# Expert layer: the 64-token tiles of two experts in one output tile, and weights loaded by pairs

## The reference, cut to what matters

```
dispatch   = jnp.einsum('sec,sd->ecd', sec_mask.astype(tokens.dtype), tokens)   # 16 x 320 x 128
h          = jax.nn.gelu(jnp.einsum('ecd,edf->ecf', dispatch, w1))              # w1: 16 x 128 x 512
expert_out = jnp.einsum('ecf,efd->ecd', h, w2)                                  # w2: 16 x 512 x 128
out        = jnp.einsum('sec,ecd->sd', combine_weights.astype(tokens.dtype), expert_out)
```

## Time and profile before

| | before |
|---|---|
| median of 3 runs | 884.03 us (880.08 to 884.72) |
| the profiled execution | 883.63 us |
| its span | 881.9 us |
| TensorE busy | 775.9 us, 88% of the span |
| VectorE, ScalarE, GpSimd busy | 527.1, 467.3, 306.0 us |
| DMA | 78.05 MB, mean 89 GB/s |
| second products L919, matmul passes | 384 records |
| weight loads of the expert stage | 24 transfers of 256 KB |

### The profile page before, as it was taken

One profiled execution on the slowest core, in us unless ns is written; L12 is line 12 of the kernel. 1 busy time (PEld: TensorE's weight loads), 2 busy tenths in 40 slices (PEclk: granted clock), 3 DMA queues, 4 the chain that ended last, 5 costly groups with the idle time before them and its releaser, 6 DMA issues.

```text
span 881.9 us, 19604 instructions
## 1 busy us (share of the span) xinstructions
PE 775.9 (88%) x7317; PEld 439.1 (50%) x7317; DVE 527.1 (60%) x1390; ACT 467.3 (53%) x743; POOL 306.0 (35%) x444
## 2 busy tenths in 40 slices
PE   1689999999928999479999999999999999999993
PEld 0234444444316777424555555555555555565441
DVE  4448888888441122255776647776665876545666
ACT  1487898889811222125544435554444555455575
POOL 3122443343337000234444325443334433224405
PEclk9999999999958999769999999999999999999997
DMA  1276333333205544131443244543335444222003
GB/s 28 75 236 157 105 98 103 106 101 97 64 31 130 153 141 140 54 89 49 103 100 71 52 88 103 103 102 72 70 73 96 103 91 92 56 55 54 2 1 96
DMA packets 111706, 78.05 MB, mean 89 GB/s; under 512 B 12272, under 2 KB 103088, under 8 KB 111616
## 3 DMA queue, kind: packets, MB, share of 16 engines
q1 hardware_dynamic: 106256, 70.38, 33.1%
q0 software_dynamic: 3344, 5.56, 2.5%
q10 hardware_dynamic: 2016, 0.92, 0.4%
HBM read 37.86 MB, written 13.63 MB: 58 GB/s over the span
## 4 chain that ended last, share of the span: by engine, by line
PE 34%; SPq 9%; DVE 6%; DMA 3%; issue 2%; ACT 1%; POOL 1%; ACTq 0%; DVEq 0%; POOLq 0%
PE l_ps_v L1287 7%; PE l_ps_c L1260 7%; SPq L115 4%; SPq L113 4%; PE l_ps_v L1188 4%; PE l_ps_d L1273 3%; PE l_by_query L1209 2%; DMA q_ring<-l_max_rows 2%; DVE l_rden L1839 2%; PE l_by_query L1200 2%; PE l_by_key L1242 1%; DVE l_neg_max L1827 1%; PE l_by_key L1380 1%; PE l_ps_m L1177 1%; PE l_ps_m L1380 1%
## 5 line engine op out<-in xcount | busy, mean ns | idle before, releaser
L1827 DVE TENSOR_REDUCE l_neg_max<-l_by_query 128x6 bf16<-128x768 f32 x125 | 119.7, 957 | 126.3 <-PE l_by_query L1213 125.6
L2107 POOL TENSOR_SCALAR_AFFINE_SELECT l_probs<-l_probs 128x512 f32<-128x512 f32 x128 | 88.2, 689 | 202.7 <-ACT l_probs L1533 202.4
L1533 ACT ACTIVATE l_probs<-l_by_key 128x768 f32<-128x768 f32 x128 | 103.8, 811 | 69.6 <-PE l_by_key L1245 65.4
L490 ACT ACTIVATE l_probs<-l_ps_s,minus_bound 128x1024 f32<-128x1024 f32 x128 | 137.2, 1118 | 2.4 <-PE l_ps_s L364 2.3
L1260 PE MATMUL l_ps_c<-l_probs,l_values 128*64 128x256 f32 (+1 forms) x1024 | 112.0, 340 | 0.0
L1260 PEld LDWEIGHTS l_ps_c<-l_probs,l_values 128*64 128x64 f32 x1024 | 62.3, 136 | 38.8 <-issue 19.6
L379 PE MATMUL l_ps_o<-l_probs,l_vpad 128*32 128x256 f32 x1024 | 78.9, 390 | 0.2 <-ACT l_probs L490 0.2
L1188 PE MATMUL l_ps_v<-w_v,l_xT 128*128 128x512 f32 x128 | 73.6, 657 | 0.4 <-ACT l_values L1554 0.4
L1554 ACT ACTIVATE l_values<-l_ps_v 128x512 f32<-128x512 f32 x64 | 38.2, 597 | 66.9 <-PE l_ps_v L1188 64.5
L1287 PE MATMUL l_ps_v<-w_o,l_ctx 128*128 128x128 f32 x512 | 66.9, 285 | 0.0
L2115 POOL DMA_INDIRECT l_eg<-eout_d,fetch x32 | 34.4, 1076 | 90.3 <-POOLq L836 82.7
(11 more groups left out here) (263 smaller groups left out, 1438.0 us busy)
## 6 DMA issues: line engine op xcount, KB each, us to landing
l_rrep<-rden_d SPq DMA_DIRECT2D x32, 512.0 KB
q_ring<-l_parts SPq DMA_DIRECT2D x192, 64.0 KB
k_ring<-l_parts SPq DMA_DIRECT2D x180, 64.0 KB
w_both<-in_L_ffn_w_dram SPq DMA_DIRECT2D x32, 256.0 KB, 3.1
disp_d<-zeros SPq DMA_DIRECT2D x8, 320.0 KB, 3.5
l_xin<-in_L_attn_x_dram SPq DMA_DIRECT2D x16, 128.0 KB, 2.5
l_xr<-in_L_attn_x_dram SPq DMA_DIRECT2D x16, 128.0 KB, 2.4
x_d<-l_x SPq DMA_DIRECT2D x16, 128.0 KB, 2.1
```

Of the source, the lines that this page charges most:

```text
L490: act.activation(probs[c % RING][:, :], ps_s[c % 2][:, :], ACT.Exp, bias=k["minus_bound"][:, :], scale=SCALE).then_inc(probs_sb, 1)
L1533: act.activation(probs[c % P_RING][:, :, 0:N + P], by_key[:, :, 0:N + P], ACT.Exp, scale=SCALE).then_inc(p_sb, 1)
L1827: dve.tensor_reduce(neg_max[:, :, half, :, h].rearrange("p a u -> p u a"), query_scores(b, c)[:, :, 0:3 * P].rearrange("p u (a q) -> p u a ...
L2107: pool.affine_select(out=corners, in_=corners, compare_op=ALU.is_ge, fill=0.0, base=0, pattern=[[0, 4], [1, P]], channel_multiplier=-1).th ...
```

## The change

The 64-token tile is left out of even steps. In odd step e it is computed for both experts of the pair, e-1 into partitions 0 to 63 and e into partitions 64 to 127 of one output tile, in alternating matmuls. `hT` has four buffers instead of two (the two new ones lie in memory that the second layer uses later). Full tiles are copied and stored each step, the shared tile (`y_rest`) once a pair by one copy of 128 x 128 and two transfers of 32 KB. The weights of two experts are loaded together after odd steps: e+3 first, then e+4.

```diff
-        ye_parts = [(slice(0, P), slice(0, FULL))] + ([(slice(0, CAP % P), slice(FULL, FULL + 1))] if CAP % P else [])
+
+        def copies(he, q):
+
+            return he * 6 + (1, 3, 4, 6)[q]
...
                 if real(e):
-                    wait_apart(sp, k, (y_sb, (e + 1) * len(ye_parts)))
-                    for dram, sbuf in tiles(eout_d, e, ye[p]):
-                        sp.dma_start(dram, sbuf).then_inc(ye_out[p], 16)
-                if real(e) and real(e + W):
+                    wait_apart(sp, k, (y_sb, copies(he, q)))
+                    full = rows(eout_d, e, 0, FULL * P).rearrange("(t p) c -> p t c", p=P)
+                    sp.dma_start(full, ye[p][:, :, :]).then_inc(ye_out[p], 16)
+                    if p == 1:
+                        sp.dma_start(rows(eout_d, e - 1, FULL * P, REST), y_rest[0:REST, :]).then_inc(rest_out, 16)
+                        sp.dma_start(rows(eout_d, e, FULL * P, REST), y_rest[REST:P, :]).then_inc(rest_out, 16)
+                if real(e) and real(e + W) and p == 1:
 
                     wait_apart(sp, k, (y_ps, e + 1))
-                    sp.dma_start(w1_sb[q][:, :], expert(w1, e + W)).then_inc(w_in[q], 16)
-                    sp.dma_start(w2_sb[q][:, :, :], expert(w2, e + W).rearrange("(f p) c -> p f c", p=P)).then_inc(w_in[q], 16)
+                    for d in (1, 0):
+                        sp.dma_start(w1_sb[q - d][:, :], expert(w1, e + W - d)).then_inc(w_in[q - d], 16)
+                        sp.dma_start(w2_sb[q - d][:, :, :], expert(w2, e + W - d).rearrange("(f p) c -> p f c", p=P))\
+                          .then_inc(w_in[q - d], 16)
...
                     pe.wait_ge(h_sb, (e + 1) * 2)
-                    at_least(pe, y_sb, (e - 1) * len(ye_parts))
-                    for t, n in TILES:
+                    if q >= 2:
+                        pe.wait_ge(y_sb, copies(he, q - 2))
+                    elif not isinstance(e, int) or e >= 2:
+                        pe.wait_ge(y_sb, copies(he - 1, q + 2))
+                    for t in range(FULL):
                         for f in range(FC):
-                            last = pe.matmul(ps_y[p][0:n, t // P * C:(t // P + 1) * C], hT[p][:, f, t:t + n],
+                            last = pe.matmul(ps_y[p][:, t * C:(t + 1) * C], hT[q][:, f, t * P:(t + 1) * P],
                                              w2_sb[q][:, f, :], start=f == 0, stop=f == FC - 1)
+                    if p == 1:
+                        for f in range(FC):
+                            for d, half in ((1, slice(0, REST)), (0, slice(REST, P))):
+                                last = pe.matmul(ps_y[1][half, FULL * C:(FULL + 1) * C], hT[q - d][:, f, FULL * P:CAP],
+                                                 w2_sb[q - d][:, f, :], start=f == 0, stop=f == FC - 1)
                     last.then_inc(y_ps, 1)
...
-                    at_least(dve, ye_out[p], LOADS * half(0))
-                    for r, c in ye_parts:
-                        dve.tensor_copy(ye[p][r, c, :], ps_y[p][r, c.start * C:c.stop * C].rearrange("p (t c) -> p t c", c=C))\
-                           .then_inc(y_sb, 1)
+                    at_least(dve, ye_out[p], 16 * half(0))
+                    dve.tensor_copy(ye[p][:, :, :], ps_y[p][:, 0:FULL * C].rearrange("p (t c) -> p t c", c=C)).then_inc(y_sb, 1)
+                    if p == 1:
+                        at_least(dve, rest_out, 32 * half(0))
+                        dve.tensor_copy(y_rest[:, :], ps_y[1][:, FULL * C:(FULL + 1) * C]).then_inc(y_sb, 1)
```

More of the change, by code:

```diff
@@ L835, in experts @@
     FULL = CAP // P
+    REST = CAP % P
+    assert 2 * REST == P
     with ExitStack() as ctx:
@@ L842, in experts @@
         xeT = [sb(f"xeT{i}", [P, CAP], FP32) for i in two]
+        later = k["x3"][:, :, :].rearrange("p a b -> p (a b)")
         hT = [sb(f"hT{i}", [P, FC, CAP], FP32) for i in two]
-        ye = [sb(f"ye{i}", [P, len(TILES), C], FP32) for i in two]
+        hT += [later[:, i * FC * CAP:(i + 1) * FC * CAP].rearrange("p (f n) -> p f n", n=CAP) for i in two]
+        ye = [sb(f"ye{i}", [P, FULL, C], FP32) for i in two]
+        y_rest = sb("y_rest", [P, C], FP32)
         ps_x = pb("ps_x", [P, 512], FP32)
@@ L848, in experts @@
         xe_in, ye_out = [sem(f"xe_in{i}") for i in two], [sem(f"ye_out{i}") for i in two]
+        rest_out = sem("rest_out")
         cleared, later_in, rows_set = (sem(n) for n in ("cleared", "later_in", "rows_set"))
@@ L867, in experts, with rows @@
         LOADS = 16 * len(list(tiles(disp_d, 0, xe[0])))
-        ye_parts = [(slice(0, P), slice(0, FULL))] + ([(slice(0, CAP % P), slice(FULL, FULL + 1))] if CAP % P else [])
+        def copies(he, q):
+            return he * 6 + (1, 3, 4, 6)[q]
+        def rows(dram, e, first, n):
+            return dram[e * CAP + first:e * CAP + first + n, :] if isinstance(e, int) else dram[bass.ds(e * CAP + first, n), :]
         @block.sync
@@ L878, in step @@
                 if real(e):
-                    wait_apart(sp, k, (y_sb, (e + 1) * len(ye_parts)))
-                    for dram, sbuf in tiles(eout_d, e, ye[p]):
-                        sp.dma_start(dram, sbuf).then_inc(ye_out[p], 16)
-                if real(e) and real(e + W):
+                    wait_apart(sp, k, (y_sb, copies(he, q)))
[5 more added lines that the diff above has]
+                if real(e) and real(e + W) and p == 1:
                     wait_apart(sp, k, (y_ps, e + 1))
-                    sp.dma_start(w1_sb[q][:, :], expert(w1, e + W)).then_inc(w_in[q], 16)
-                    sp.dma_start(w2_sb[q][:, :, :], expert(w2, e + W).rearrange("(f p) c -> p f c", p=P)).then_inc(w_in[q], 16)
+                    for d in (1, 0):
+                        sp.dma_start(w1_sb[q - d][:, :], expert(w1, e + W - d)).then_inc(w_in[q - d], 16)
+                        sp.dma_start(w2_sb[q - d][:, :, :], expert(w2, e + W - d).rearrange("(f p) c -> p f c", p=P))\
+                          .then_inc(w_in[q - d], 16)
             pipelined(sp, step, 3, 0, E, W)
             for i in two:
-                sp.wait_ge(ye_out[i], LOADS * E // 2)
+                sp.wait_ge(ye_out[i], 16 * E // 2)
+            sp.wait_ge(rest_out, 32 * E // 2)
         @block.tensor
@@ L927, in step @@
             def step(e, he, q):
-                o = 1 - q % 2
                 if real(e + 1):
@@ L932, in step @@
                         at_least(act, y_ps, e)
-                        act.activation(hT[o][:, 2 * i:2 * i + 2, :], ps_h[i][:, :, 0:CAP], ACT.Gelu_apprx_tanh).then_inc(h_sb, 1)
+                        act.activation(hT[(q + 1) % W][:, 2 * i:2 * i + 2, :], ps_h[i][:, :, 0:CAP], ACT.Gelu_apprx_tanh).then_inc(h_sb, 1)
             pipelined(act, step, 2, 0, E, W, first=1)
```

## The result

The changed kernel is slower: median 895.90 us of 11 runs (887.21 to 900.45) against 884.94 us of 11 runs before (880.08 to 889.11). The ratio is 1.0115, 95% interval 1.0089 to 1.0140: about 11 us. The profiled execution takes 900.04 us, near the slow end of the eleven; its span is 898.3.

What follows compares the result with a forecast made beforehand. TensorE was taken to bound the expert stage. Second products -8.7 us, weight waits +12.0, token waits +0.75, stage end +0.5 and clock falls +3.3 gave +7.8 on 883.63: 891.4 us, range 884.5 to 898.

Steps and rivals of the forecast that it cites:

- What bounds the kernel: Expert stage: TensorE is busy 57.60 of 57.60 us over ten steps and sets the step of 5.76 us.
- the halves' gain: Second products: even steps shrink to 4.67 us, odd ones stay at 5.76 as paired halves run together; TensorE saves 8.7 us.
- The third rival: Odd steps' shared tile: halves don't run together or weight loads aren't hidden; 900 us, chance 0.03.
- The wait for weights: Before first products of steps 3 to 13, odd: six TensorE waits of 1.85 or 2.15 us, 2.0 in the mean.
- T: The end of an odd step e on TensorE, from which issue and landing times of the loads are counted.
- The wait for tokens: Tokens of expert e+4, queued behind four weight loads: no wait without the turn, 0.25 us three times with it, +0.75 us.
- the turn: The unrolled loop's turn, behind odd steps 3, 7 and 11; tokens forecast to land at T + 8.5 without it.
- The clock: TensorE's clock falls to 0.50 behind two of six weight waits, about 1.6 us each: +3.3 us.
- the fourth rival: Expert stage: the same waits and no fall of the clock; 888.1 us, chance 0.27.
- the second rival: Expert stage: the same waits, and the clock falls behind all or nearly all; 897.7 us, chance 0.17.
- The rival on the other side: Odd steps 3 to 13: weights land in time; with no wait at all 875.4 us, chance 0.08.

Runs made afterwards that it cites:

- e1: The changed kernel without the weight loads of experts 4 to 15, which so use the first four experts' weights: 875.52 us, ratio 0.9885 to the kernel before.
- e2: The changed kernel with the tokens of expert e+4 issued between the two pairs of weights, not behind both: 894.14 us, ratio 1.0101 to the kernel before.
- after_again: The changed kernel run once more, unaltered, for a second profile: 888.88 us beside 878.41 for the kernel before on that chip, ratio 1.0121.
- e8: The changed kernel with 8 idle identity matmuls before the wait for weights of odd steps 3 to 13: 889.06 us, ratio 1.0124 to the kernel before.
- e4: The changed kernel with w1 loaded every step, w2 on its own counter, tokens issued ahead of outputs and weights: 875.71 us, ratio 0.9901 to before.
- e6: The changed kernel with all four matmuls of one half issued before the four of the other: 896.94 us, ratio 1.0139 to the kernel before.
- e3: The changed kernel with w1 loaded every step, only w2 in pairs on its own counter, tokens behind the weights: 889.84 us, ratio 1.0060 to before.
- e9: e2 with 8 idle identity matmuls before the wait for weights of odd steps: 884.75 us, ratio 1.0076 to the kernel before.

## Why the prediction was right, and where it was off

**What bounds the kernel, and the halves' gain: right.** Even steps of 4.66 us (forecast 4.67) and a shared tile of 1.03 us. The gain was 9.7 instead of 8.7, since odd steps became 0.10 shorter too.

**The third rival, weight loads that are not hidden: refuted.** e1 and the changed kernel run both halves with their 16 weight loads (133 to 137 ns each, 2.2 us together) inside 1.03 us, as the earlier trace rows had it.

**The wait for weights: right in place, cause and number, and nearly in size.** There are six waits before the first products of odd steps, 1.90 to 2.17 us (forecast 1.85 and 2.15 in turn), ended by the weights' DMA. w2 was issued at T + 3.60 (T + 3.52) and landed 3.1 us later. TensorE started 0.2 us after the landing (320.9 to 321.14), which the forecast had left out: that is the 13.2 against 12.0. VectorE's copies did not keep their number, as the forecast says: they are three a pair instead of four (x1382 against x1390 in the page). No wait of TensorE in the stage names them.

**The wait for tokens: right in kind, mis-sized; this is the term that failed.** "Landing 2.8 later" and "no wait" without the turn took a landing time from the kernel before, where one pair of weights is issued just ahead of the tokens, and not two. The earlier trace rows showed landings growing in a row. The loads issued at 318.51, 318.96, 319.58 and 320.15 (time to landing, each queried by itself) read:

```profile
w_both<-in_L_ffn_w_dram SPq DMA_DIRECT2D x1, 256.0 KB, 3.8
w_both<-in_L_ffn_w_dram SPq DMA_DIRECT2D x1, 256.0 KB, 4.9
ex_xe<-disp_d SPq DMA_DIRECT2D x1, 128.0 KB, 3.7
ex_xe<-disp_d SPq DMA_DIRECT2D x1, 32.0 KB, 4.3
```

The last tokens land at T + 10.2 (320.15 + 4.3), not at T + 8.5: issued 0.2 us later than forecast, and 1.5 us longer on their way. That makes six waits of 1.15 us instead of three of 0.25, or 6.9 us against 0.75. e2 shows that it is the place in the queue: issued ahead of the second pair, the tokens cost no wait.

**The clock: right in kind, too much for this kernel.** Falls do follow such waits. One of 3.4 us cost 1.6 to 1.7 us in e2 (forecast 1.6), and the one of 6.8 us in after_again made its step 2.4 us longer than its like. But in the changed kernel they stand behind one of twelve waits, not two of six, and e8 finds no price in the median. The first profile is in this what the fourth rival said: the same waits and no fall. Its 888.1 us would have been short by the 6 us of the tokens. That the total came near is luck: this term was 3.3 us too large where the tokens' was 6.1 too small. The Trainium skill (TensorE: Matmul & The Clock Gate, "HAM oscillation") tells of a kernel in which every wait on DMA between bursts of matmuls set the clock back. Its waits are longer than any here, and the forecast read it as if it said the same of waits of 2 us. In the changed kernel one of twelve did, so the second rival did not come true.

**The rival on the other side** (weights in time) is what e4 makes true by another route; forecast without a wait 875.4 us, measured 875.7.

## What to carry to other kernels

An engine that is made faster in one step asks for its inputs earlier in the next: before shortening a step, list what was issued so many steps ahead that it was never late, and count again with the shorter step. When work of two steps is merged, only the operands of the merged part have to live longer; load the others on their own counter and at their old time. And where several transfers are queued at once, put the small one that is wanted first ahead, and price the ones behind by landing times with as much in flight ahead of them, never by those of a shorter queue.

## What the runs showed of the hardware

- Matmuls into the two halves of the array overlap even if all of one half's are issued first (e6): 16 passes in 1.52 us, against 1.03 us in alternation.
- After idle times of TensorE between 1.7 and 2.3 us the clock may or may not fall: 1.71 us was followed by 0.50 (e3), 2.21 was and 2.22 was not (both e2), 2.23 was not (e3). Length alone does not decide it.
- With matmuls of no use in the waits the clock stayed at 1.00 in the stage, in twelve waits of two profiles. They cost next to nothing when they fit inside (even steps of 6.99 us in e9 against 6.94 in e2), and e9's stage is 100.8 us against 105.9.
- A megabyte of weights in one burst moves more slowly than its start suggests: the first pair landed in 2.8 and 3.1 us, the second, issued 1.2 us later, in 3.8 and 4.9, and 32 KB of tokens behind them in 4.3.
